# Narrow attentions with 512 keys: two heads' scores on 64 rows of the array each, instead of one head on all 128

## The reference, cut to what matters

```python
# L2 (L3 is alike, with biases, a normalisation ahead and an MLP behind)
Q = (hidden @ Wq.T).reshape(B, Tt, 16, 16).transpose(0, 2, 1, 3)
K = (a @ Wk.T).reshape(B, Ta, 16, 16).transpose(0, 2, 1, 3)
V = (a @ Wv.T).reshape(B, Ta, 16, 16).transpose(0, 2, 1, 3)
scores = jnp.where(mask, einsum('bhtd,bhsd->bhts', Q, K) * scale, -inf)   # 2 x 16 x 256 x 512
attn = softmax(scores, axis=-1)
out = einsum('bhts,bhsd->bhtd', attn, V) ... @ Wo.T
```

## Time and profile before

| | us |
|---|---|
| median of 3 runs | 1091.75 |
| lowest, highest | 1088.05, 1092.27 |
| the profiled execution | 1090.92 |
| its span in the profile | 1089.1 |
| mean granted clock of TensorE | 0.944 |
| TensorE, VectorE, ScalarE, GpSimd busy in it | 952.1, 777.3, 604.8, 312.8 |

### The profile page before, as it was taken

One profiled execution on the slowest core, in us unless ns is written; L12 is line 12 of the kernel. 1 busy time (PEld: TensorE's weight loads), 2 busy tenths in 40 slices (PEclk: granted clock), 3 DMA queues, 4 the chain that ended last, 5 costly groups with the idle time before them and its releaser, 6 DMA issues. The chain is left out here.

```text
span 1089.1 us, 17930 instructions
## 1 busy us (share of the span) xinstructions
PE 952.1 (87%) x6616; PEld 807.3 (74%) x6616; DVE 777.3 (71%) x1627; ACT 604.8 (56%) x1369; POOL 312.8 (29%) x321
## 2 busy tenths in 40 slices
PE   4888886789999999998899999998588899779958
PEld 4766665679988898987688989888467666556657
DVE  3486766458877887886678878777683688667864
ACT  3587873236555555553355556555443788267842
POOL 3454540050221122221111222200004456345510
PEclk8899998999999999998899999999878899889989
DMA  4996006140110011111000111000213940394020
GB/s 149 268 233 88 2 2 230 31 147 1 39 39 4 37 40 39 40 39 39 1 4 37 40 39 39 2 1 1 74 47 111 232 63 2 98 236 70 4 84 20
DMA packets 39490, 72.71 MB, mean 67 GB/s; under 512 B 6534, under 2 KB 23944, under 8 KB 37228
## 3 DMA queue, kind: packets, MB, share of 16 engines
q1 hardware_dynamic: 39404, 71.56, 24.7%
...
## 5 line engine op out<-in xcount | busy, mean ns | idle before, releaser
L1312 ACT CAST L1a_probsT_hi<-L1a_bank 128x512 fp32r<-128x512 f32 x128 | 68.8, 590 | 94.3 <-PE L1a_bank L1190 94.3
L1148 POOL TENSOR_SCALAR L1a_wo_hi<-L1a_stage 128x512 fp32r<-128x512 f32 x16 | 10.4, 651 | 362.4 <-PE L1a_sums L74 355.2
L1346 ACT ACTIVATE L1a_probs<-L1a_scores,L1a_neg_max 128x512 f32<-128x512 f32 x128 | 87.0, 685 | 30.9 <-DVE L1a_bias_shifted L1435 26.0
L1431 DVE TENSOR_REDUCE L1a_top<-L1a_scores 128x2 f32<-128x1024 f32 x64 | 78.2, 1223 | 34.7 <-PE L1a_scores L74 34.6
L1369 DVE TENSOR_TENSOR L1a_probsT_lo<-L1a_bank,L1a_probsT_hi 128x512 fp32r<-128x512 f32 x128 | 82.0, 682 | 0.1
L72 PE MATMUL L1a_bank<-L1a_probsT_hi,L1a_v_hi 128*128 128x256 f32 x256 | 73.1, 286 | 9.2 <-DVE L1a_probsT_lo L1369 9.2
L1314 ACT ACTIVATE L1a_attended_hi<-L1a_bank,L1a_cols 128x256 fp32r<-128x256 f32 x64 | 30.5, 476 | 90.3 <-PE L1a_bank L74 90.3
L72 PE MATMUL L1a_bank<-L1a_w_hi,ctxT_hi 128*128 128x256 f32 x256 | 75.8, 296 | 1.1 <-DVE L1a_k_lo L1371 1.1
L417 POOL TENSOR_SCALAR L0a_probs<-L0a_probs,L0a_inverse 128x768 f32<-128x768 f32 x64 | 57.4, 909 | 57.9 <-DVE L0a_inverse L686 57.9
L73 PE MATMUL L1a_bank<-L1a_w_lo,ctxT_hi 128*128 128x256 f32 x256 | 73.2, 286 | 0.0
L74 PE MATMUL L1a_bank<-L1a_w_hi,ctxT_lo 128*128 128x256 f32 x256 | 73.1, 286 | 0.0
...
## 6 DMA issues: line engine op xcount, KB each, us to landing
...
```

The source lines that it names most:

```text
L1312: nc.scalar.copy(out, source).then_inc(ring.hi_done, 1)
L1346: nc.scalar.activation(probs[:, g % 2, qt, :], scores[:, qt, :], ACT.Exp, bias=neg_max[:, g % 2, qt:qt + 1], accum_out=row_sum[:, g % 2, q ...
L1431: link(nc.vector.tensor_reduce(top[:, :], scores[:, :, :], AX.X, ALU.max))
```

## The change

- `q_stack` has one version of each pair, not two; every preset value in it is 1.0 (one memset of 128x1024 per buffer in place of one of 128x2048 and two of 32x1024).
- The score matmuls contract over 64 rows: a step g now makes the scores of both heads a of pair g // 2, for query tile g % 2. The two heads use rows 0 to 63 and 64 to 127 of the array and write to two slots of PSUM. Both wait until both exponentials of step g - 2 are done.
- A head's two query tiles come two steps apart (`made`, `nth`), so transposes wait for another count, and LAG is 4, not 3. There are 12 slots of probabilities and of small values, not 8.
- `spoiled` is worked out for steps 0 and 1 of a batch in place of step 0 alone.

```diff
@@ -227,11 +227,14 @@
 
         k_stack = [ph.sb("k_stack", [P, 4, nk], F32R),
                    w_qkv[:, :, :, :].rearrange("p s i n -> p (s i n)")[:, 0:4 * nk].rearrange("p (t n) -> p t n", t=4)]
-        q_stack = [ph.sb(f"q_stack{i}", [P, 2, 4, Q], F32R) for i in range(2)]
-
-        score_slots, probs_slots, small_slots = (4, 8, 8) if nk == S else (2, 6, 8)
+
+
+        beside = nk == S
+        q_stack = [ph.sb(f"q_stack{i}", [P, 1 if beside else 2, 4, Q], F32R) for i in range(2)]
+
+        score_slots, probs_slots, small_slots = (4, 12, 12) if beside else (2, 6, 8)
         probs = ph.sb("probs", [P, probs_slots, nk])
-        spoiled = ph.sb("spoiled", [P, 2])
+        spoiled = ph.sb("spoiled", [P, 2, 2])
         TSLOTS = 5
         probsT = ph.sb("probsT", [P, TSLOTS, 2 * nkt * P])
 
@@ -298,7 +301,7 @@
             return src[part][:, kt, at:at + n]
 
 
-        LAG = 3 if nk == S else 2
+        LAG = 4 if nk == S else 2
 
         def product_before(t):
 
@@ -314,6 +317,12 @@
                     order.append(("B", 0, 0))
             order += [("T", t, c) for c in range(tj)]
         order.append(("V", units - 1, 0))
+
+        def made(m):
+
+            return (m // 4 * 2 + m % 2, m // 2 % 2) if beside else (m // 2, m % 2)
+
+        nth = {made(m): m for m in range(2 * HEADS)}
 
         def slot_scores(m):
             return scores[:, m % score_slots, 0:nk]
@@ -361,7 +370,7 @@
                 if o == 1:
                     for other in range(1, OCTETS):
                         write(other)
-                sp.wait_ge(cleared[r], 3)
+                sp.wait_ge(cleared[r], 2 if beside else 3)
                 if o == 0:
                     sp.wait_ge(mask_written, 16)
                 if o >= 2:
@@ -374,7 +383,7 @@
                 for a in range(2):
                     rows = slice(64 * a, 64 * a + 48)
                     sp.dma_start(raw(k_stack[r][rows, :, :]), k_dram[o, a:8:2, :, :, :].rearrange("t r c n -> (r c) t n")).then_inc(stack_loaded[r], 16)
-                    sp.dma_start(raw(q_stack[r][rows, a, :, :]), q_dram[o, a:8:2, :, :, :].rearrange("t r c n -> (r c) t n")).then_inc(stack_loaded[r], 16)
+                    sp.dma_start(raw(q_stack[r][rows, 0 if beside else a, :, :]), q_dram[o, a:8:2, :, :, :].rearrange("t r c n -> (r c) t n")).then_inc(stack_loaded[r], 16)
                 if o == 1 and cfg["bias_values"]:
                     for other in range(2, OCTETS):
                         sp.wait_ge(written[other], 96)
@@ -403,11 +412,14 @@
                     nc.gpsimd.memset(padding, 0.0).then_inc(padding_set, 1)
                     if cfg["bias_values"]:
                         nc.gpsimd.memset(spread[:, :, :, :], 0.0).then_inc(spread_clear, 1)
-                nc.gpsimd.memset(raw(q_stack[r][:, :, :, :]), 0.0).then_inc(zeroed, 1)
-                pool.wait_ge(zeroed, r + 1)
-                for a in range(2):
-                    nc.gpsimd.memset(raw(q_stack[r][64 * a + 32:64 * a + 64, a, :, :]), 1.0).then_inc(cleared[r], 1)
-                pool.wait_ge(cleared[r], 2)
+                if beside:
+                    nc.gpsimd.memset(raw(q_stack[r][:, :, :, :]), 1.0).then_inc(cleared[r], 1)
+                else:
+                    nc.gpsimd.memset(raw(q_stack[r][:, :, :, :]), 0.0).then_inc(zeroed, 1)
+                    pool.wait_ge(zeroed, r + 1)
+                    for a in range(2):
+                        nc.gpsimd.memset(raw(q_stack[r][64 * a + 32:64 * a + 64, a, :, :]), 1.0).then_inc(cleared[r], 1)
+                    pool.wait_ge(cleared[r], 2)
                 if r:
                     pool.wait_ge(ring.full, u0)
                 nc.gpsimd.memset(raw(k_stack[r][:, :, :]), 0.0).then_inc(cleared[r], 1)
@@ -465,14 +477,14 @@
                 last.then_inc(ring.full, 1)
 
             def transpose_head(g):
-                pe.wait_ge(normed, 2 * g + 2)
+                pe.wait_ge(normed, max(nth[g, 0], nth[g, 1]) + 1)
                 for c in range(tj):
                     job = job_of["T", g, c]
                     ring.wait_bank(pe, job)
                     for i in range(4):
                         qt, kt = divmod(4 * c + i, nkt)
                         last = nc.tensor.transpose(ring.bank(job)[:, i * P:(i + 1) * P],
-                                                   probs[:, (2 * g + qt) % probs_slots, kt * P:(kt + 1) * P], keep["ident"][:, :])
+                                                   probs[:, nth[g, qt] % probs_slots, kt * P:(kt + 1) * P], keep["ident"][:, :])
                     last.then_inc(ring.full, 1)
 
             def product_v(unit):
@@ -497,14 +509,22 @@
                     r = octet % 2
                     if e == 0:
                         pe.wait_ge(stack_loaded[r], 16 * stack_dmas * (octet // 2 + 1))
-                    for qt in range(2):
-                        m = 2 * g + qt
-                        if m >= score_slots:
-                            pe.wait_ge(exp_done, m - score_slots + 1)
-                        for c0, n in [(0, S)] + ([(S, extra)] if extra else []):
-                            last = nc.tensor.matmul(slot_scores(m)[:, c0:c0 + n], q_stack[r][:, e % 2, e // 2, qt * P:(qt + 1) * P],
-                                                    k_stack[r][:, e // 2, c0:c0 + n], start=True, stop=True)
-                        last.then_inc(scores_full, 1)
+                    if beside:
+                        if 2 * g + 1 >= score_slots:
+                            pe.wait_ge(exp_done, 2 * g + 2 - score_slots)
+                        for a in range(2):
+                            half, qt = np.s_[64 * a:64 * a + 64], g % 2
+                            nc.tensor.matmul(slot_scores(2 * g + a), q_stack[r][half, 0, e // 2, qt * P:(qt + 1) * P],
+                                             k_stack[r][half, e // 2, :], start=True, stop=True).then_inc(scores_full, 1)
+                    else:
+                        for qt in range(2):
+                            m = 2 * g + qt
+                            if m >= score_slots:
+                                pe.wait_ge(exp_done, m - score_slots + 1)
+                            for c0, n in ((0, S), (S, extra)):
+                                last = nc.tensor.matmul(slot_scores(m)[:, c0:c0 + n], q_stack[r][:, e % 2, e // 2, qt * P:(qt + 1) * P],
+                                                        k_stack[r][:, e // 2, c0:c0 + n], start=True, stop=True)
+                            last.then_inc(scores_full, 1)
                 if t >= 0:
                     if product_before(t) is not None:
                         product_v(product_before(t))
@@ -601,7 +621,7 @@
                         small = m % small_slots
                         act.wait_ge(max_done, m + 1)
                         if m >= probs_slots:
-                            act.wait_ge(ring.full, job_of["T", (m - probs_slots) // 2, tj - 1] + 1)
+                            act.wait_ge(ring.full, job_of["T", made(m - probs_slots)[0], tj - 1] + 1)
                         nc.scalar.activation(probs[:, m % probs_slots, :], slot_scores(m), ACT.Exp,
                                              bias=neg_max[:, small:small + 1],
                                              accum_out=row_sum[:, small:small + 1]).then_inc(exp_done, 1)
@@ -677,12 +697,13 @@
                     if 2 * g - 2 >= small_slots:
                         dve.wait_ge(normed, 2 * g - small_slots)
                     sums = row_sum[:, small:small + 2]
-                    if cfg["nan_if_masked"] and (g - 1) % H == 0:
-
-
-                        link(nc.vector.tensor_scalar(spoiled[:, :], neg_max[:, small:small + 2], -MASKED, 0.0, ALU.mult, ALU.mult))
-                        link(nc.vector.tensor_tensor(spoiled[:, :], spoiled[:, :], sums, ALU.add))
-                        sums = spoiled[:, :]
+                    if cfg["nan_if_masked"] and (g - 1) % H < (2 if beside else 1):
+
+
+                        own = spoiled[:, (g - 1) % 2, :]
+                        link(nc.vector.tensor_scalar(own, neg_max[:, small:small + 2], -MASKED, 0.0, ALU.mult, ALU.mult))
+                        link(nc.vector.tensor_tensor(own, own, sums, ALU.add))
+                        sums = own
                     nc.vector.reciprocal(inverse[:, small:small + 2], sums).then_inc(inverse_done, 1)
                 if t >= 0:
                     if product_before(t) is not None:
```

## The result

| | before | changed |
|---|---|---|
| median of 20 runs each, by turns on one chip (us) | 1089.79 | 1093.49 |
| lowest, highest | 1086.52, 1093.61 | 1088.93, 1100.62 |
| ratio, with its 95% interval | | 1.0039 (1.0027 to 1.0051) |
| profiled execution, its span | 1090.92, 1089.1 | 1097.03, 1095.2 |
| mean granted clock of TensorE | 0.944 | 0.941 |

What follows compares the result with a forecast made beforehand. VectorE and ScalarE by turns were taken to bound the loops. Tails +3.7, first V -0.2 and -0.5, memsets -0.3 made +2.7 us on the profiled 1090.92: 1093.6 us, range 1087.5 to 1101.

Steps and rivals of the forecast that it cites:

- the memsets: Front of L3a: smaller GpSimd memsets let the first cast end earlier, -0.3 us, bounds 0 and -0.9; in L2a 0.
- the pairing: Score matmuls on 64 rows in both loops: 0.20 us of TensorE time saved a step, under slack, so 0.
- The pace: Both loops: VectorE and ScalarE by turns set 1.86 us a step, 3.56 with V; TensorE has slack.
- the rival that TensorE becomes the bound: Every step of both loops: dearer array switches take TensorE's unit past 9.14 us; 1102.5 us, chance 0.16.
- the one that the step with V shrinks by itself: Steps with V: VectorE's wait of 1.21 us goes away in 12 steps; 1079.1 us, chance 0.13.
- The switches of the array: TensorE around each score pair: seven more changes of shape a unit, 0.15 us each, held by slack, so 0.
- The rival of a half clock in all steps: Both loops: TensorE's clock falls to half, its unit takes 13.9 us; about 1151 us, chance 0.04.
- The tail, +1.85 a loop: End of each loop: V of unit 6 waits for ScalarE's later copy of head 27; +3.7 us for two loops.
- E31: First exponential of step 31, at each loop's end; V of unit 6 was to start 2.13 us behind it, before 0.28.
- The start: Steps 4 to 7 come a microsecond or so earlier, but step 8 waits for its DMA, so nothing is gained.
- The first V: Second octet: the first V comes in step 9, not 8; -0.2 us in L2a, -0.5 in L3a.
- the upper bound of +0.7: First V of L3a, in the second octet: if V is slow too, the change there is +0.7 us.

Runs made afterwards that it cites:

- experiment 7: The changed kernel with each pair of score matmuls issued twice into the same slots; ratio to before 1.0014, median 1090.89 us.
- experiment 6: The changed kernel with VectorE's low half of the product behind its copy in steps with V; ratio to before 1.0018, median 1092.42 us.
- experiment 10: The kernel before with ScalarE's high half of the product between the two exponentials in steps with V; ratio 0.9942, median 1084.13 us.
- experiment 1: The kernel before with LAG 4 and 12 slots, still 128-row scores and old memsets; ratio 1.0046, median 1097.17 us.
- experiment 4: The changed kernel with ScalarE's copy of head 27 ahead of step 31's exponentials; ratio to before 1.0013, median 1092.66 us.
- experiment 3: The changed kernel with GpSimd's memsets held until VectorE has split the transposed queries; ratio to before 0.9996, median 1091.50 us.
- experiment 12: The changed kernel with GpSimd waiting for its q_stack memset before it issues k_stack's; ratio to before 1.0023, median 1093.95 us.
- experiment 5: The kernel before with GpSimd's memsets held until VectorE has split the transposed queries; ratio 1.0004, median 1090.39 us.
- experiment 9: The kernel before with LAG 4, 12 slots and late memsets, still 128-row scores; ratio 1.0034, median 1094.99 us.

## Why the prediction was right, and where it was not

The forecast was 1093.6 us and the median is 1093.49. That is better than its reasons: it started from 1090.92, 1.1 us over the median of the kernel before in these runs (1089.79), and its change of +2.7 was 1.0 to 1.5 us too small. Within that change two more errors of opposite sign cancel, the memsets and the pairing. To be right to 0.1 us was luck; the mechanism of the loop and the tail was not.

- **The pace** (VectorE and ScalarE by turns, not TensorE): right. 1.85 and 3.56 us stay, experiment 7 adds TensorE work to every step and changes no pitch, and experiments 6 and 10 shorten the step with V by program order alone. So the rival that TensorE becomes the bound is out, and so is the one that the step with V shrinks by itself.
- **The switches of the array**, taken as +0.15 each and -0.20 a pair, so +0.06 us a step (7.68 against 7.43 over four steps): measured +0.18 ahead of a pair and -0.12 behind it, +0.06. The slack held them, as forecast. The two matmuls of a pair start 1 to 4 ns apart (0.31 us or more before) and both are over in the 0.50 us of one, so they do run side by side.
- **The clock in the loop**: 1.00 from 880 to 900 in the changed kernel too. The rival of a half clock in all steps is out. Its cousin at the gaps is real, though: a tail with LAG 4 leaves TensorE idle for 1.14 and 0.86 us ahead of V of unit 6, and in two profiled tails that V took 3.6 us. That may be why the changed kernel's runs spread to 1100.62; no run separates it.
- **The tail, +1.85 a loop**: right to the hundredth (E31 to V7 5.81 to 7.67), and the copy named as its cause is confirmed by experiments 1 and 4.
- **The start**: S8 waits for its DMA as before, and the head start is lost there, as forecast. The first V was forecast at -0.2 in L2a (measured -0.14 from S8 to E10) and -0.5 in L3a; there it is +0.36, because V too ran at the slow clock (3.06 us): the case from which the upper bound of +0.7 was worked out. Over more profiles the sign is as forecast: S0 to E10 is 1.0 us shorter in L2a and 1.8 in L3a (means of changed, 3, 4 and 12 against before and 5).
- **`spoiled`**: right. The one in the step with V is hidden (the wait of 1.21 becomes 0.81), the other costs 0.4 as before.
- **The memsets: the step that failed.** "I take -0.3 in L3a, bounds 0 and -0.9." The wrong sign: the cast path became 1.74 us longer. I had costed the removed instructions and not the removed waits. With them gone the long k_stack memset was in line when the short one ended, and it passed the waiting cast; I had priced only the second cast's delay behind it. Putting one wait back restores 4.13 us (experiment 12), and taking all memsets out of the way gives 4.7 us by the runs (experiment 3), of which 2.1 to 2.9 are seen in the front, part of it through the clock.
- **The pairing: counted 0, gives 2.5 to 4.1 us back** (experiment 12 against 1, 9 against 3). I looked at its steady state, where it is 0, and not at what an earlier or later end of step 7 does to TensorE's gap before S8 and to the clock behind it.

By the runs LAG 4 alone is between +3.3 (experiment 9 less experiment 5) and +5.0 (experiment 1), where +3.0 was forecast; the memsets +1.7 to +4.7, where -0.3 was forecast; the pairing -2.5 to -4.1, where 0 was forecast. That the parts from experiments 5, 9 and 3 add up to 4.2 proves nothing, since they are differences along one chain. The stages are a second account: tails +3.7, front of L3a +2.6 (28.51 less 25.88), S0 to E10 of both loops -2.8, in all +3.5 of the 4.2. The last two terms are means over a few profiles each, and single ones differ by over 1 us with the clock.

The Trainium skill, "SBUF — State Buffer", "SBUF: two separate sides", says that VectorE's two-port operations and GpSimd share one pair of ports, that who starts first holds it for the whole instruction, and that the other blocks. The rows agree: each blocked cast ends some 0.28 us behind the end of a memset (948.17 behind 947.89; 950.19 behind 949.91), and the memset behind it is longer by as much (2.08 instead of 1.80). That section says nothing on who comes next when a cast is waiting and a second memset is in line; the changed kernel's rows show the memset at 946.14 and the cast at 947.89 and 949.91, and experiment 12 shows the cast at the first of these places when GpSimd waits in between.
